# A decoder layer's self attention, rebuilt: two heads and the position bias in one score product, queries stacked by transfers

## What is computed

```python
q = (hidden_states @ Wq).reshape(b, s, NUM_HEADS, HEAD_DIM)
kv = hidden_states @ Wkv
k, v = (kv[..., :HEAD_DIM], kv[..., HEAD_DIM:])
scores = jnp.einsum('bqhd,bkd->bhqk', q, k) * scale
bias = slopes[:, None, None] * (pos[None, None, :] - pos[None, :, None])
scores = jnp.where(causal[None, None], scores + bias[None], -jnp.inf)
attn = jax.nn.softmax(scores, axis=-1)
out = jnp.einsum('bhqk,bkd->bqhd', attn, v).reshape(b, s, h)
return out @ Wo
...
x = x + _L0_attn_ref(_layernorm(x, axis=-1), L0_attn_Wq, L0_attn_Wkv, L0_attn_Wo)
x = x + _L0_xattn_ref(_layernorm(x, axis=-1), ctx_4096, ctx_4096, ...)
x = x + _L0_ffn_ref(_layernorm(x, axis=-1), L0_ffn_W_gate, ...)
```

## Time and profile before

| what | value |
|---|---|
| time of the kernel, median of 3 runs | 1030.61 us (1030.24 to 1031.05) |
| span of the profiled execution | 1029.7 us |
| first scores product of the self block | 19.66 us |
| first product of the cross block | 236.36 us |
| PE, DVE, ACT, POOL busy, share of the span | 97%, 56%, 42%, 37% |

### The profile page before, as it was taken

One profiled execution on the slowest core, in us unless ns is written; L12 is line 12 of the kernel. 1 busy time (PEld: TensorE's weight loads), 2 busy tenths in 40 slices (PEclk: granted clock), 3 DMA queues, 4 the chain that ended last, 5 costly groups with the idle time before them and its releaser, 6 DMA issues. The chain is left out here.

```text
span 1029.7 us, 16071 instructions
## 1 busy us (share of the span) xinstructions
PE 1003.1 (97%) x5260; PEld 822.9 (80%) x5260; DVE 581.3 (56%) x973; ACT 428.1 (42%) x1239; POOL 381.6 (37%) x375
## 2 busy tenths in 40 slices
PE   5999999989999999999999999999999999999998
PEld 3787777876888888888888888888887778888787
DVE  3765555636776666767666666766765852222101
ACT  2777666751533433533533434434334433332100
POOL 7422222253642642643634534626424222222100
PEclk8999999989999999999999999999999999999999
DMA  6000000211110210210210201201100022221001
GB/s 199 12 11 11 11 10 10 62 52 52 50 54 1 73 32 0 71 31 0 74 27 20 72 10 31 61 10 49 43 1 32 1 62 61 61 69 47 11 31 41
DMA packets 45699, 39.98 MB, mean 39 GB/s; under 512 B 3617, under 2 KB 34465, under 8 KB 45665
## 3 DMA queue, kind: packets, MB, share of 16 engines
q1 hardware_dynamic: 45280, 38.48, 12.7%
q0 software_dynamic: 384, 1.05, 0.3%
HBM read 37.43 MB, written 2.10 MB: 38 GB/s over the span
## 5 line engine op out<-in xcount | busy, mean ns | idle before, releaser
L624 PE MATMUL bank<-cross_wo_hl,cross_outT_hl 128*128 128x512 f32 x768 | 191.7, 398 | 1.0 <-POOL cross_wo_hl L618 0.6
L624 PE MATMUL bank<-hsT_hl,cross_wqkv_hl 128*128 128x512 f32 x768 | 188.2, 394 | 0.0
L624 PEld LDWEIGHTS bank<-cross_wo_hl,cross_outT_hl 128*128 128x128 f32 x768 | 143.1, 188 | 35.5 <-POOL cross_wo_hl L618 1.6
L624 PEld LDWEIGHTS bank<-hsT_hl,cross_wqkv_hl 128*128 128x128 f32 x768 | 141.9, 188 | 29.3
L938 ACT ACTIVATE cross_scores<-cross_scores,cross_negmax 128x128 f32<-128x128 f32 x256 | 99.8, 391 | 127.1 <-DVE cross_negmax L876 127.1
L798 POOL TENSOR_TENSOR cross_qT<-rotated,rotated_other_half 128x512 f32<-128x512 f32 x64 | 82.8, 1293 | 162.0 <-DVE rotated_other_half L840 162.0
L624 PE MATMUL bank<-hsT_hl,ff_gate_upT_hl 128*128 128x512 f32 (+1 forms) x528 | 126.3, 395 | 0.5 <-DVE ff_gate_upT_hl L1140 0.5
L624 PEld LDWEIGHTS bank<-hsT_hl,ff_gate_upT_hl 128*128 128x128 f32 (+1 forms) x528 | 96.3, 186 | 21.9 <-DVE ff_gate_upT_hl L1140 0.8
L948 ACT CAST cross_outT_hl<-bank 128x512 fp32r<-128x512 f32 x64 | 37.1, 579 | 143.4 <-PE bank L624 142.5
L838 DVE TENSOR_TENSOR rotated<-bank,cosT 128x512 f32<-128x512 f32 x80 | 55.2, 690 | 71.4 <-PE bank L624 71.2
L624 PE MATMUL bank<-ctxT_hl,cross_wqkv_hl 128*128 128x512 f32 x384 | 94.3, 394 | 1.1 <-PEq L74 1.1
(11 more groups left out here) (121 smaller groups left out, 1565.7 us busy)
## 6 DMA issues: line engine op xcount, KB each, us to landing
staged_rows<-in_wq SPq DMA_DIRECT2D x32, 256.0 KB, 2.8
staged_rows<-in_wo SPq DMA_DIRECT2D x32, 256.0 KB, 2.7
staged_rows<-in_wg SPq DMA_DIRECT2D x10, 256.0 KB, 2.6
staged_rows<-in_wu SPq DMA_DIRECT2D x10, 256.0 KB, 2.8
staged_rows<-in_wd SPq DMA_DIRECT2D x10, 256.0 KB, 3.0
ctx_tok<-in_ctx SPq DMA_DIRECT2D x8, 256.0 KB, 2.6
staged_rows<-in_wk SPq DMA_DIRECT2D x8, 256.0 KB, 3.1
staged_rows<-in_wv SPq DMA_DIRECT2D x8, 256.0 KB, 3.1
```

What stands on the lines that cost most here:

```text
L624: i = nc.tensor.matmul(out, stationary[:, a], moving[:, b], start=(first and k == 0), stop=(last and k == 2))
```

## The change

Only the self block and its tables are new; the two other blocks stay as they were.

- Queries are projected transposed, for four sequences at a time: a high-and-low product with the weights stationary (L499 of the new kernel), once for four rows of features. Before the attention begins, this is done for sequences 0 to 3; for sequences 4 to 7 it is done in steps of sequences 2 and 3.
- The contraction of a score product holds two heads: for each head 16 rows high, 16 rows low, 16 rows high again, and 16 rows of slope and position terms that carry the bias. 24 transfers for each sequence (`load_q`, 16 partitions x 4 x 128 values, 32 KB each, from SBUF to SBUF) stack the queries so, into one of two rings of `self_q_by_pair`. They are issued by SP. The score product is then one pass of 256 columns for two heads.
- VectorE adds a mask only. The exponential also gives its row's sum; VectorE inverts it in each step, and GpSimd scales the probabilities before the transposes.
- Values: for 16 heads at a time, four products of 32 columns x 512, each written to a quarter of one bank's partitions (`values`); two of them accumulate the 32 heads. The result is already transposed, so the transposes of the output go.
- The output product is a high-and-low one. The context comes transposed from the host, in eight chunks (`load_ctx`), and ScalarE and GpSimd split it in steps of sequences 4 and 5.

```diff
+CTX_CHUNKS = {(b, s): 4 * (b - 4) + s // 2 for b in (4, 5) for s in (1, 3, 5, 7)}
...
+            def load_q(b):
+
+                half, at = b // HALF, (b % HALF) * P
+                sp.wait_ge(sem["bank_read"], use_of("q", HALF * half + HALF - 1) + 1)
+                if b >= RINGS:
+                    sp.wait_ge(sem["scores1"], STEPS * (b - RINGS + 1))
+                for hh in range(8):
+                    for copy, part in enumerate((0, 1, 0)):
+                        to = 64 * (hh % 2) + HD1 * copy
+                        sp.dma_start(qT[to:to + HD1, b % RINGS].rearrange("p (c r) k -> p c r k", r=QUAD)[:, :, hh // 2, :].bitcast(F32),
+                                     q_hl[HD1 * hh:HD1 * hh + HD1, part, :, at:at + P].bitcast(F32)).then_inc(sem[f"q_loaded{b % RINGS}"], 16)
+
+            def load_ctx(j):
+                if j >= 2:
+                    sp.wait_ge(sem["ctx_low"], j - 1)
...
             load_ctx(0)
-            with sp.Fori(1, SEQS) as b:
-                sp.wait_ge(sem["ctx_transposed"], b)
-                load_ctx(b)
+            load_ctx(1)
+            load_q(4)
+            for j in range(2, 5):
+                load_ctx(j)
+            load_q(5)
+            for j in range(5, 8):
+                load_ctx(j)
             for j in range(PIECES):
+                if j == 0:
+                    sp.wait_ge(sem["wo1_low"], QUAD)
+                if j == SLOTS:
+                    load_q(6)
+                    load_q(7)
                 load_piece(sp, m, sem, j, j % SLOTS, piece_source(io, j, 0), first=j < SLOTS)
...
+            def scores(n):
+                b, s = n // STEPS, n % STEPS
+                if s == 0:
+                    pe.wait_ge(sem[f"q_loaded{b % RINGS}"], Q_DMAS * (b // RINGS + 1))
...
+                for k in range(2):
+                    e = nc.tensor.matmul(SC[n % 2][:, k * 2 * P:(k + 1) * 2 * P], qT[:, b % RINGS, 2 * s + k, :], kexp[:, b, :], start=True, stop=True)
...
+            def values(w):
+
+                b, second = w // 2, w % 2
+                pe.wait_ge(sem["probsT1"], QUAD * w + QUAD)
...
+                for j in range(QUAD):
+                    e = nc.tensor.matmul(OB[32 * j:32 * j + 32, :], v[:, b, 0:32] if second else v[:, b, 16:48],
+                                         PT[:, (QUAD * w + j) % SLOT_PT], start=not second, stop=bool(second))
```

More of the change, by code:

```diff
@@ new lines, in last_of, with bank_uses, use_of, highs_before @@
+def last_of(kind):
+    return 3 if kind in ("q", "kv", "out") else 0
+def bank_uses():
+    uses = [(kind, i) for kind, i, tiles in before_attention()]
+    for b in range(SEQS + 1):
+        for s in range(STEPS):
+            uses += [(kind, i) for kind, i, tiles in steps_in(b, s) if last_of(kind) in tiles]
+    return uses
+USES = bank_uses()
+def use_of(kind, i):
+    return USES.index((kind, i))
+def highs_before(u):
+    return sum(1 for kind, i in USES[:u] if kind != "out")
+def ended_in(b, s):
+    if s == 0:
+        b, s = b - 1, STEPS
+    return [(kind, i) for kind, i, tiles in steps_in(b, s - 1) if last_of(kind) in tiles] if b >= 0 else []
@@ L213, in _ @@
             pool.wait_ge(sem["pos_loaded"], 16)
-            pool.wait_ge(sem["q1"], SEQS)
             for b in range(SEQS):
@@ L414, in body @@
-                    if s == 5 and back and not scores:
-                        for i in range(HALF):
-                            act.wait_ge(sem["tables_transposed"], i + 1)
-                            t = ps[i][:].rearrange("p (b w k) -> p w b k", b=2, w=2)
-                            nc.scalar.copy(m["cosT"][:, 2 * i * P:2 * (i + 1) * P].rearrange("p (b k) -> p b k", b=2), t[:, 0])
-                            nc.scalar.copy(m["sinT"][:, 2 * i * P:2 * (i + 1) * P].rearrange("p (b k) -> p b k", b=2), t[:, 1])
@@ L576, in _ @@
-            with pe.Fori(3, SEQS - 1) as b:
-                body(b)
-            for b in range(SEQS - 1, SEQS + 1):
-                body(b)
+                    if n + 1 < STEPS * SEQS:
+                        scores(n + 1)
+                    if n >= 3:
+                        transposes(n - 3)
+                    if n >= 7 and n % QUAD == 3:
+                        values(n // QUAD - 1)
+                    for kind, i, tiles in steps_in(b, s):
+                        step(kind, i, tiles)
@@ L582, with attnT_low @@
+            for n in range(STEPS * SEQS - 3, STEPS * SEQS):
+                transposes(n)
+            values(2 * SEQS - 1)
+            step("out", SEQS - 1, (0, 1, 2, 3))
+def attnT_low(nc, dve, sem, attnT, OB, b):
+    dve.wait_ge(sem["attnT_high"], b + 1)
+    nc.vector.tensor_tensor(attnT[:, 1], OB[:], attnT[:, 0].bitcast(F32), ALU.subtract).then_inc(sem["attnT_low"], 1)
 PIECES = 6
```

798 lines of the change are left out of this document (386 added, 412 removed).

## The result

The changed kernel takes 1075.76 us (median of 4 executions, 1071.78 to 1076.13) beside 1030.42 before (4 executions, 1029.58 to 1031.05): ratio 1.043, 95% interval 1.0412 to 1.0449. It is slower by 45.3 us; 16.3 were forecast, and the time lies outside the range. The profiled execution took 1076.08 us with a span of 1074.1; the span before was 1029.7, 44.4 less.

A forecast was written before the change was run, and what follows sets the result against it. TensorE was taken to bound the kernel, ScalarE to take over. Start plus 24.1, 64 steps minus 11.4, end plus 3.6 make 16.3 more: 1030.6 + 16.3 = 1047 us; range 1026 to 1065, the forecast's own 1034 to 1058.

The forecast's parts named there:

- sequence 1: Self block steps with keys, values and mask: 20.7 us, taking step by step the longer engine.
- end: From the last exponentials to the self block's end: 17.9 us instead of 14.3, plus 3.6.
- the price of one set of queries: 24 transfers issued one by one by SP: 24 x 0.46 + 2.2 = 13.2 us, bounds 9.9 and 16.5.
- 7 us for the steps: Allowance for the 64 steps, used with the transfer price bounds for the forecast's own range, 1034 to 1058 us.
- The "1.9" and "1.8" us behind a set: Scores, mask and maximum between a late set's arrival and the first exponentials: 1.9 us ahead of sequence 4, 1.8 elsewhere.
- Before sequences 1, 2, 3 and 7 it costs nothing: Query sets there lie beside a sequence's steps, 18.5 us or more, so their 13.2 us are hidden.
- the sum of the steps: The 64 steps without waits for queries: 162.4 us, 37.5 less than 199.9.
- The start: Four sequences normalised and projected first, then queries sent: first exponentials at 45.9 us instead of 21.84, plus 24.1.
- The 2.5 us for slow first passes: In the start's query projections, 2.5 us beyond 11.0 for 48 passes, first passes running at half pace after idling.
- Rival 1: Quarters of a value product run one after another, 3.9 us: 10 us and 2 at the end, 1059 us; chance 0.2.
- Rival 2: Small transfers issue much cheaper; break-even 0.29 us apiece, at 0.20 the kernel takes 1024 us, faster; chance 0.12.
- Rival 3: Steps outlast either engine's sum as VectorE and ScalarE wait mutually: 0.3 us in 48 steps, 14 us, 1061; chance 0.13.

The follow-up runs named there:

- The order of the scores: Against the changed kernel, a sequence's first scores stand behind the transposes and values of the last step before it on TensorE: 1065.89 us.
- the run of the three orders: Changed kernel with context chunks on GpSimd's queue, next sequence's first scores last on TensorE, sixth weight piece last on ScalarE: 1030.67 us, ratio 1.0002 to the kernel before.
- after: The changed kernel itself, against the kernel before: 1075.76 us, ratio 1.043.
- the run with 8 transfers: Against the changed kernel, each query set is sent as 8 transfers of 48 partitions in place of 24 of 16: 1032.96 us.
- the first run with two queues: Against the changed kernel, the first query set goes 15 transfers by SP and 9 by ScalarE's queue: 1073.82 us.
- the run with two queues: The run of the three orders plus the first set over two queues and output weights loaded at the start: 1028.26 us, ratio 0.9964 to the kernel before.

## Why the prediction was wrong in size

Direction and main mechanism held: the steps are faster, and late sets of queries on the path cost more than that saves. The size was off by 28 us (44.4 between the spans, 16.3 forecast). Half of that is the price of a set; the other half is mostly waits that the sum left out or priced too low. Step by step, in us (a sequence lasts from its first exponentials to those of the next; these start at 52.97, 75.09, 98.86, 122.60, 151.67, 189.34, 224.98 and 243.11, and the last end at 262.37):

| step | forecast | measured | off |
|---|---|---|---|
| projections begin | 15.9 | 18.68 | +2.8 |
| to the first query issue | 15.0 | 15.06 | +0.1 |
| first set | 13.2 | 16.88 | +3.7 |
| scores to first exponentials | 1.8 | 2.35 | +0.5 |
| sequence 1 | 20.7 | 23.77 | +3.1 |
| sequence 2 | 19.6 | 23.73 | +4.1 |
| sequence 3 | 23.9 | 29.08 | +5.2 |
| sequence 4 | 32.4 | 37.66 | +5.3 |
| sequence 5 | 29.4 | 35.64 | +6.2 |
| sequences 0, 6, 7 | 62.5 | 59.5 | -3.0 |
| end | 17.9 | 18.0 | +0.1 |

- **The step that failed: the price of one set of queries**, 24 x 0.46 + 2.2 = 13.2 us with an upper bound of 16.5. It is 16.7 to 16.9, just outside the bounds: 24 issues 0.64 apart make 15.4, and the scores come 1.5 behind the end of the last. Four sets on the path make 14 of the 28 us. The rows it came from the earlier trace rows were loads from memory; no row showed one tile sent to another. And the 0.46 was the gap between the first four issues of a row in which the next gaps are longer, 0.48 and twice 0.55 (the kernel before, behind the 2.12 of the earlier trace rows):

```profile
2.60 0.51 SPq L118 DMA_DIRECT2D self_wq<-in_wq  x1
3.15 0.51 SPq L119 DMA_DIRECT2D x<-in_x  x1
3.70 0.56 SPq L120 DMA_DIRECT2D positions<-in_pos  x1
```

  The range was also narrower than its own bounds: four sets at 16.5 us alone make 1060, not 1058, and with 7 us for the steps 1067.
- **The "1.9" and "1.8" us behind a set** ahead of sequences 4, 5 and 6: measured 5.0, 4.9 and 5.6. The chain was taken as scores, mask, maximum. But the waiting scores stand ahead of the last transposes of the running sequence on TensorE, and ScalarE's exponentials of its last step stand behind their copy, so that step comes after the stall too. The prediction named what waits behind the scores and left this out: 10.0 us in all. The order of the scores gave back 7.7 of them; the other 2.3 are the chain itself, 2.6 us instead of 1.8 to 1.9. The sets were issued 1.1 to 1.4 us sooner than forecast, -3.9 in all.
- **"Before sequences 1, 2, 3 and 7 it costs nothing"**: for the set of 3 wrong. Its cover was taken to be the steps up to its own scores; but ScalarE has to overwrite the tile that it is read from ahead of the fourth exponentials of sequence 2, and waits 4.30 us.
- **Sequence 1**: the step with the second keys was costed by its engines' sums. TensorE has them ahead of the next scores, waits 2.56 us for VectorE's last normalised sequence, then runs the six passes in 2.85 us, where the run of the three orders took 1.58 (after, then that run):

```profile
75.60 2.85 PE L629 MATMUL bank<-hsT_hl,self_wkv_hl 128*96 128x512 f32 x6 [2.56 <-DVE hsT_hl L317]
```

```profile
74.56 1.58 PE L627 MATMUL bank<-hsT_hl,self_wkv_hl 128*96 128x512 f32 x6 [2.27 <-DVE hsT_hl L312]
```

  Sequences 0, 6 and 7 came out 3.0 us below the forecast, so in the sum of the steps, 162.4 for 158.6, errors cancel in part.
- **The start**: projections began 2.8 late. The first weights reached ScalarE at 9.57, and VectorE's two low parts took 3.42 us instead of 1.4, while GpSimd worked on the other two (3.23 us for two, where one took 1.29 in the earlier trace rows). The 2.5 us for slow first passes held: 48 passes took 13.69, 2.7 more than 11.0. But the rows that it was read from the earlier trace rows show 0.75 beside 0.49 us a pass, one and a half times and not twice.
- **Rival 1** (quarters one after another) is refuted: eight passes in 1.06 us, and 1.94 at the lower clock, both below the 2.4 taken. The Trainium skill (TensorE: Matmul & The Clock Gate, Why this matters for your kernels), which has products in different column quarters run side by side, agrees. **Rival 2** (cheap issues) is refuted by 0.595 us, and its break-even too, since the other terms cost more than forecast: with 8 transfers a set lasts 7.2 us, less than the 9.2 of 24 issues at 0.29, and the kernel still ends 2.6 us behind before. **Rival 3** (long steps) is refuted by 158.6 us without query waits. As forecast are ScalarE's idle 5.25 us at the end and the cross block's unchanged length.

The kernel lost because it bought 41 us of faster steps (199.9 to 158.6) with 51 us of waits for late queries and of what stands behind these (209.4 from the first exponentials to the end of the last, beside 158.6 without the late sets), a start that is 31 us later, in which one more set stands, and an end that is 3.7 longer.

## What to carry to other kernels

A tile that is rearranged by many small transfers is priced by transfers times issue time on the queue that sends them; from 16 to 48 partitions the size made no difference here. Take the issue time from transfers of that kind sent in a row. Merge them (43 us in the run with 8 transfers, though its output is not the reference's), let nothing that waits stand ahead of them on their queue (37 us here), or spread them over queues (4 us of the first set here). When a wait is added, follow not only the waiting instruction but all that stands behind it in every in-order list, to the last step of the work that was already under way. And keep large loads out of the moment in which small ones are waited for, but not so late that someone waits for them in turn.

## What was not expected of the hardware

- SP's issue of a transfer from one SBUF tile to another took 0.585 us at the least, 0.595 in the median, for 16 partitions with 64 runs of 512 bytes; the median was 0.589 for 16 runs of 2048 and 0.609 for 48 partitions. ScalarE's queue took 0.618, GpSimd's 0.514 for the same transfers. Loads from memory on SP took 0.33 to 0.43 in the earlier trace rows, but not everywhere: in after one behind a pause took 0.33 (context chunks at 157.24, 161.78 and 167.30), five weight pieces in a row 0.43 to 0.58, and one right behind a query transfer 0.59 (the 1 MB at 41.50 in the first run with two queues). A query transfer took 0.59 even behind a pause (129.99). Why was not settled. The five pieces:

```profile
199.83 0.43 SPq L606 DMA_DIRECT2D staged_rows<-in_wk  x1
200.30 2.23 SPq L606 DMA_DIRECT2D staged_rows<-in_wq  x4
```

- The same six passes of the second key product (96 columns of weights, 512 moving) took 2.85 us in after and 1.58 in the run of the three orders. The two stretches, in the order of the columns above:

```profile
75.60:78.20 2.60, 2.60 (x6) 1.80 (x7) 1.31 (x3) 1.16 (x7) 1.04 (x1) 0.50 0.25 51
```

```profile
74.60:76.10 1.50, 1.50 (x8) 1.12 (x8) 1.28 (x3) 1.12 (x6) 0.09 (x1) 1.00 0.25 50
```

  The granted clock was 0.50 (1.2 GHz) in the one and 1.00 (2.4 GHz) in the other, behind 2.56 and 2.27 us in which TensorE did nothing. Why it fell in one and not in the other was not settled; it is worth 1.3 us here, and 2.2 in the run with two queues, where both halves ran at the slower level's pace.
